# A two-layer graph kernel: in layer 1, TensorE picks two row tiles in place of one in every fourth step

## The chip, the cores and the metric

The kernel runs on one core of one Trainium2 chip. A core has five engines that run side by side and wait for each other by semaphores: TensorE (PE; matmuls into the eight banks of PSUM), VectorE (DVE), ScalarE (ACT), GpSimd (POOL) and SyncE (SP), and 16 DMA engines that move data between HBM and the on-chip memory SBUF. The metric is the device time of one execution in microseconds (us).

## The reference, cut to what matters

There are 12500 nodes with 32 features and 212500 edges, sorted by target. Layer 0 is an edge network with a segment maximum. Layer 1, the one that is changed, is a relational attention:

```python
x = h[src]                                    # one row of h for each edge
y = h[dst]
c = w_comp[etype]
msg = einsum('eb,ebo->eo', c, einsum('ei,bio->ebo', x, weight))
x_hat = x @ A1_w.T + A1_b
y_hat = y @ A2_w.T + A2_b + rel_emb[etype]
a = tanh(relu(sum(x_hat * y_hat, -1) / sqrt(32)))
nei = segment_sum(a[:, None] * msg, dst)
```

Each layer is added to its input, and a layer norm follows. The gather `h[src]` is where the change lies: how the rows of h come to the edges.

## The kernel before, in words

The edges lie in four streams. A step takes 512 edges of each, 2048 in all, as 16 row tiles of 128 edges with 32 features; each layer has 104 steps. A step's source rows come into one of two slots of the tile `xg1` in layer 1. The trace calls `xg1`, `xs` and the room of the hot tiles `rows_in`, because they share one tensor.

**How a row tile comes in.** Most come by a gather that GpSimd issues (L763): one indirect DMA for each row tile. Some are "hot": TensorE picks them with a one-hot matrix. The node of an edge is split into a class (which of 7 x 128 groups) and a lane (which of 14 nodes in the group). The one-hot matrix of the classes, 7 x 128 x 128 in bf16, is built by VectorE in layer 0 (`class_hot`), saved to HBM by SP (`hot_save`, L609) and loaded again in layer 1 (`hot_load`, L615). 21 matmuls (7 classes times 3 bf16 parts of h) give, for each edge, the 14 x 32 values of its group in one PSUM bank. VectorE multiplies them by a lane mask (`mask_hot`, L1369) and sums over the lanes (`add_hot`, L1375) into `xg1`. In layer 1 the last of the 16 row tiles is hot in each step from 6 to 101, so 15 are gathered.

**A step of layer 1.** Each engine runs a written-out order. For step s TensorE does, in this order:

- coefficients 0 and 1 (`coef`, L1591: matmuls that spread a coefficient over the features, in three banks in turn; each waits for the product that last read its bank)
- the score's sum (`score_sum`, L1608, bank 1), coefficient 2, the last messages of step s-1 (L1600), coefficient 3
- `compose` for step s+1 (L1617, banks 0 and 1), coefficient 4, the turn of the target rows (L1482), coefficient 5, `relate` for step s+1 (L1629, bank 5), coefficients 6 and 7
- the turn of the source rows of step s+1 (`source_turn`, L1648), which waits for its gathers and hot rows; coefficients 8 and 9
- hot piece 0 for step s+2 (`hot_rows`, L1664), messages of k = 0, coefficient 10, messages of k = 1, hot piece 1, coefficients 11 and 12, the key of step s+1 (`find_key`, L1672)
- hot piece 2, coefficient 13, hot piece 3, coefficient 14, hot piece 4, coefficient 15, hot piece 5, messages of k = 2, the turn of the sums of step s-1 (L1492)

`PIECES1` says where the 21 matmuls are cut into these six pieces. The first matmul of a tile waits for the hot load and for the query of step s+1, because the tile is summed in bank 5, which the query reads.

VectorE does in step s: the mask of the hot tile of step s+1, product 0 (`product`, L1340: the source features times a coefficient), the sum over the lanes, products 1 to 4, the weighing of the messages of step s-1 (L1347), product 5, a scan (L1353), product 6, a scan for step s+1 (L1235), product 7, the query of step s+1 (`find_query`, L1323), products 8 to 13, the lane mask of step s+2 (L1361), products 14 and 15, the score of step s+1 (`find_score`, L1329).

ScalarE copies what TensorE has turned to `xs` and stores it to HBM (L972). SP loads it back four times as `x4` (L723), which product 0 of the next step needs. SP's queue runs in order; for step s it loads indices, one-hot types, target rows, flags, the hot tile (L615), and then x4 for step s-2. GpSimd starts the gathers of step s when the slot has been turned and copied, that is two steps ahead of their use, and paces them by TensorE's coefficients.

Of the kernel before, what the change touches and what calls it, by code (L numbers as in the profile page):

```python
# [23 lines left out]
F = 32  # L24
# [34 lines left out]
LAST_HOT1 = STEPS - 2  # L59
FEW_HOT = STEPS - 5  # L60
PIECES = {1: (2, 4), 2: (5, 8), 3: (7, 12)}
HOTS1 = (1,)
PIECES1 = {1: (0, 0, 6, 11, 11, 16, 21)}
PICK = 14
CLASSES = NODES // (PICK * P)
HOT_COLS = STEPS * HOT
# [63 lines left out]
def hot1_count(n):  # L130

    if not FIRST_HOT1 <= n < LAST_HOT1:
        return 0
    return HOTS1[n % len(HOTS1)] if n < FEW_HOT else 1


def hot1_before(n):

    return sum(hot1_count(m) for m in range(n))
# [41 lines left out]
def build(nc, t):  # L181
    ctx = ExitStack()
    with ctx:
# [3 lines left out]
        def dram(name, shape, dt=fp32):  # L187
            return nc.dram_tensor(name, shape, dt, kind="Internal").ap()

        def sem(name):  # L190
            return ctx.enter_context(nc.semaphore(name))
# [13 lines left out]
        onehot_dram = dram("onehot_dram", [STEPS * TYPE_ROWS, STREAMS * LEN], bf16)  # L205
        hot_dram = dram("hot_dram", [STEPS * P, max(HOTS1) * CLASSES * P], bf16)

# [79 lines left out]
        def hot1(s):  # L287

            n = hot1_count(s.at)
            start = s.slot(2) * max(HOTS1) * CLASSES * P  # L290
            return hot1_room[:, start:start + n * CLASSES * P].rearrange("p (c t n) -> p c t n", c=CLASSES, t=n)
# [20 lines left out]
        def part(n):  # L312
            at[0] += n
            return late[:, at[0] - n:at[0]]
# [30 lines left out]
        h_low = part(NODE_COLS * F // 2).bitcast(bf16).rearrange("p (c n) -> p c n", c=CLASSES)  # L345
        picks1 = part(max(HOTS1) * PICK * F).rearrange("p (t f h) -> p t f h", f=F, h=PICK)

# [16 lines left out]
        bank = [psum[:, i, :] for i in range(8)]  # L364
        wmsg = bank[7]
        key = bank[0]
        hot_bank = [bank[6 + u][:, 0:PICK * F] for u in range(2)]
        hot_bank1 = [bank[5][:, 0:PICK * F]]

        def hot1_bank(s, t):  # L370

            return hot_bank1[t - hot1_count(s.at)]
# [65 lines left out]
        comp_ready = sem("comp_ready")  # L438
# [28 lines left out]
        hot1_read = sem("hot1_read")  # L467
# [12 lines left out]
        def wait_count(eng, s, semaphore, count):  # L480
            if s.known and count <= 0:
                return
            eng.wait_ge(semaphore, count)
# [39 lines left out]
        def wait_step(eng, s, semaphore, each=1, lag=0, more=0):  # L523

            wait_count(eng, s, semaphore, (s.at - lag + 1) * each + more)
# [31 lines left out]
        def _(sp):  # L557
# [47 lines left out]
            def hot_save(s):  # L605

                wait_step(sp, s, hot_built)
                n = max(HOTS1)
                sp.dma_start(hot_v[s.at][:, 0:n * CLASSES * P].rearrange("p (c t n) -> p c t n", c=CLASSES, t=n),  # L609
                             class_hot[s.slot(2)][:, :, HOT - n:HOT, :]).then_inc(hot_saved[s.slot(2)], 16)  # L610

# [42 lines left out]
            for n in range(PRE):  # L654
                hot_save(Step(PRE, 0, n))
                if n + 2 < PRE:
                    class_load(Step(PRE, 0, n + 2))
            sp.wait_ge(x_spread, 16 * NODE_COLS)

            def loads0(s):  # L660
                index = s.plus(PRE - 2)
                if index.exists() and (not s.known or index.at >= PRE + AHEAD):
                    index_load0(index)
                wait_step(sp, s, s_turned[0], lag=2)
                sp.dma_start(sp_in[:, s.slot(2)], spread_v[s.at]).then_inc(spread_in[0][s.slot(2)], 16)
                wait_step(sp, s, hid_done, each=2, lag=2)
                sp.dma_start(ea[:, s.slot(2), :], ea_v[s.at]).then_inc(ea_in[s.slot(2)], 16)
                keep_load(0, s)
                if hot(s.plus(4)):
                    class_load(s.plus(4))  # L670
                if hot(s.plus(2)):
                    hot_save(s.plus(2))
                if s.at >= 1:
                    types_load(s.plus(-1))
                if s.at >= 3:
                    onehot_save(s.plus(-3))
# [777 lines left out]
        def _(pe):  # L1454

            pe.wait_ge(lifted, 2)
            for k in range(NODE_COLS + 1):
# [5 lines left out]
                for q, half in enumerate(HALVES):  # L1463
                    if k >= 2:
                        pe.wait_ge((dve_counted, act_counted)[u], 2 * (k // 2) + q - 1)
                    for a in range(*half, 512):
                        b = min(a + 512, ROW)
# [137 lines left out]
            def score_sum(s):  # L1605

                wait_step(pe, s, score_ready)
                pe.matmul(bank[1][:, :], ones_blk[:, :], score, start=True, stop=True).then_inc(sum_done, 1)  # L1608

            def compose(s):  # L1610
# [41 lines left out]
            def hot_rows(s, piece):  # L1652

                each = CLASSES * PARTS
                a, b = PIECES1[hot1_count(s.at)][piece:piece + 2]
                for n in range(a, b):
                    t, rest = divmod(n, each)
                    if n == 0:
                        wait_in_hot = (s.earlier(2) - FIRST_HOT1 // 2 + 1) * 16
                        wait_count(pe, s, hot1_in[s.slot(2)], wait_in_hot)  # L1660
                    if rest == 0:
                        wait_step(pe, s, query_ready, lag=1)
                    c, q = divmod(rest, PARTS)
                    last_ = pe.matmul(hot1_bank(s, t), hot1(s)[:, c, t, :], h_parts[q][:, c, :],  # L1664
                                      start=rest == 0, stop=rest == each - 1)
                    if rest == each - 1:
                        last_.then_inc(hot1_done, 1)
# [10 lines left out]
            def step1(s):  # L1678
# [3 lines left out]
                turn = more and not turns_last and not picked_early(ahead)  # L1682
                coefs(s, 0, 2)
                score_sum(s)
                coef(s, 2)
                if behind.exists():
# [15 lines left out]
                if pick:  # L1702
                    hot_rows(later, 0)
# [3 lines left out]
                if pick:  # L1707
                    hot_rows(later, 1)
# [6 lines left out]
                if pick:  # L1715
                    hot_rows(later, 2)
# [151 lines left out]
```

## Time and profile before

| what | value |
|---|---|
| median of 3 runs | 4306.55 us (4303.88 to 4308.16) |
| the profiled execution | 4308.25 us |
| its span, first to last instruction | 4306.4 us |
| busy: PE / PE weight load / DVE / ACT / POOL | 86% / 39% / 64% / 28% / 74% |
| gathers of layer 1 (L763) | 1540, mean 946 ns |
| products of layer 1 (L1340) | 1664, mean 680 ns |
| hot matmuls of layer 1 (L1664) | 2016, mean 354 and 353 ns |

The busy shares run over both layers and the preparation. Layer 1 takes the second half of the span, from about 2200 us on. Matmuls are pipelined: the row of one shows its whole way through the array, so that rows overlap. The 0.3 us between two gathers are listed as idle by "issue": the engine waited for nothing that the profile shows.

### The profile page before, as it was taken

Reading aid. Unit: us, or ns where it says so; the run is one execution under the profiler, and the core shown is the slowest. Engines: PE = TensorE matmul, PEld = TensorE weight load, DVE = VectorE, ACT = ScalarE, POOL = GpSimd, SP = SyncE. Lnnn points to the kernel's source line nnn. Section 1 sums busy time; section 2 is a strip of 40 time slices with the busy share of each in tenths; the row PEclk is TensorE's granted clock in tenths of the full one; section 3 lists DMA queues with packets and bytes.
Section 4 is the critical chain, followed back from the end, with each engine's and each line's share of the span. In section 5 each row is a group of like instructions: output and inputs, shape, how many; then the busy total and the mean of one; then the engine's idle time right before and its main releaser. Section 6 shows DMA issues by size and latency. Waiting matters only on the chain.

```text
span 4306.4 us, 58419 instructions
## 1 busy us (share of the span) xinstructions
PE 3694.6 (86%) x20387; PEld 1663.0 (39%) x20607; DVE 2758.9 (64%) x4918; ACT 1197.9 (28%) x1615; POOL 3183.2 (74%) x3330
## 2 busy tenths in 40 slices
PE   7989999999999999941888989898889889988841
PEld 3444545545455455411433333333333333333311
DVE  8844444444444444426568888888888888888844
ACT  4424444444444434440011111111111111111111
POOL 7777777777777777767777777777777777777745
PEclk9999999999999999975899999999999999999965
DMA  8136565555555555551146666666666666666621
GB/s 341 26 92 154 137 143 136 141 138 141 140 138 141 138 140 142 134 133 35 28 112 168 169 172 168 163 169 168 164 163 171 167 165 162 173 167 164 159 60 32
DMA packets 526595, 608.78 MB, mean 141 GB/s; under 512 B 219555, under 2 KB 368576, under 8 KB 524128
## 3 DMA queue, kind: packets, MB, share of 16 engines
q1 hardware_dynamic: 374944, 439.68, 39.7%
q0 software_dynamic: 106432, 56.28, 8.5%
q10 hardware_dynamic: 44928, 109.07, 6.6%
q8 instruction: 166, 2.72, 0.3%
q14 instruction: 125, 1.02, 0.1%
HBM read 394.62 MB, written 210.03 MB: 140 GB/s over the span
## 4 chain that ended last, share of the span: by engine, by line
PE 59%; DVE 13%; DMA 10%; POOL 8%; issue 7%; ACT 2%; SPq 1%; ACTq 0%; DVEq 0%; POOLq 0%
PE psum L1506 24%; POOL rows_in L763 6%; PE psum L1542 6%; PE psum L1664 6%; DVE late L1340 5%; DMA late<-xs_dram 4%; PE psum L1600 4%; PE psum L1591 4%; DMA xs_dram<-rows_in 3%; PE psum L1744 3%; PE psum L1469 2%; POOL last_rows L763 2%; PE psum L1552 2%; PE psum L1492 2%; DVE dt_ L1235 2%
## 5 line engine op out<-in xcount | busy, mean ns | idle before, releaser
L763 POOL DMA_INDIRECT rows_in<-h_dram,src_idx x1540 | 1456.8, 946 | 476.3 <-issue 419.7
L763 POOL DMA_INDIRECT rows_in<-in_x_dram,src_idx x1392 | 1332.0, 957 | 435.7 <-issue 418.2
L1340 DVE TENSOR_TENSOR late<-late,psum 128x512 f32<-128x512 f32 x1664 | 1084.1, 680 | 360.7 <-PE psum L1591 217.4
L1506 PE MATMUL psum<-early,late 128*128 128x448 bf16 x5712 | 1130.8, 354 | 7.0 <-DVE late L1147 5.0
L1506 PEld LDWEIGHTS psum<-early,late 128*128 128x128 bf16 x5712 | 544.8, 98 | 625.3 <-issue 149.1
L1591 PE MATMUL psum<-comp,sel 128*128 128x512 bf16 x1461 | 512.2, 386 | 162.0 <-DVE late L1340 159.8
L1600 PE MATMUL psum<-late,basis 128*32 128x512 f32 x3328 | 449.0, 612 | 0.3 <-issue 0.3
L1147 DVE TENSOR_TENSOR late<-psum,lane_hot 128x448 f32<-128x448 f32 x272 | 169.9, 625 | 425.7 <-PE psum L1506 273.1
L1253 DVE TENSOR_TENSOR_SCAN scan<-fresh,scan,psum 128x512 f32<-128x512 bf16 x103 | 131.8, 1280 | 434.2 <-PE psum L1552 434.2
L1664 PE MATMUL psum<-x,rows_in 128*128 128x448 bf16 x1344 | 381.9, 354 | 0.0
L1591 PEld LDWEIGHTS psum<-comp,sel 128*128 128x128 bf16 x1664 | 155.6, 98 | 573.3 <-DVE late L1340 449.8
L993 ACT COPY early<-psum 128x512 f32<-128x512 f32 x104 | 61.0, 586 | 1053.1 <-PE psum L1492 1042.4
L1235 DVE TENSOR_TENSOR_SCAN dt_<-keep,dt_,psum 128x512 f32<-128x512 bf16 x206 | 263.0, 1277 | 60.7 <-PE psum L1482 60.3
L923 ACT ACTIVATE hid<-psum,b 128x512 f32<-128x512 f32 x208 | 131.7, 684 | 506.7 <-PE psum L1542 506.7
L1664 PE MATMUL psum<-late,rows_in 128*128 128x448 bf16 x672 | 237.5, 353 | 0.0
L1572 PE MATMUL psum<-ident,early 128*128 128x128 f32 (+1 forms) x56 | 15.6, 434 | 238.6 <-DVE early L1274 125.9
L1664 PEld LDWEIGHTS psum<-x,rows_in 128*128 128x128 bf16 x1344 | 123.9, 98 | 228.7 <-issue 139.1
L905 ACT ACTIVATE late<-late,row_id 96x2048 bf16<-96x2048 bf16 x104 | 207.2, 1992 | 0.4 <-ACT out L931 0.4
L909 ACT ACTIVATE late<-late 96x2048 bf16<-96x2048 bf16 x104 | 198.7, 1910 | 3.3
L1469 PE MATMUL psum<-late 128*128 128x512 bf16 (+1 forms) x775 | 148.4, 346 | 35.5 <-DVE late L1168 20.8
L1128 DVE TENSOR_SCALAR late<-late,class_id 128x384 bf16<-128x384 f16 (+2 forms) x728 | 175.1, 315 | 0.0
L1150 DVE TENSOR_REDUCE rows_in<-late 128x32 f32<-128x448 f32 x272 | 168.7, 620 | 9.4
(159 smaller groups left out, 4285.9 us busy)
## 6 DMA issues: line engine op xcount, KB each, us to landing
late<-xs_dram SPq DMA_DIRECT2D x416, 256.0 KB
sp_in<-spread SPq DMA_DIRECT2D x208, 256.0 KB
sum_rows<-early ACTq DMA_DIRECT2D x104, 512.0 KB, 2.7
late<-type_dram SPq DMA_DIRECT2D x104, 384.0 KB, 8.0
onehot_dram<-late SPq DMA_DIRECT2D x104, 384.0 KB
late<-onehot_dram SPq DMA_DIRECT2D x104, 384.0 KB
spread<-late SPq DMA_DIRECT2D x16, 1664.0 KB, 39.7
ea<-in_edge_t SPq DMA_DIRECT2D x104, 256.0 KB
```

The costliest lines, as they stand in the source:

```text
L763: pool.indirect_dma_start(out=out, out_offset=None, in_=table, in_offset=bass.IndirectOffsetOnAxis(ap=index, axis=0)).then_inc(done, 16)
L905: act.activation(gap[0:TYPE_ROWS, u], types[0:TYPE_ROWS, u], ACT.Square, bias=row_id[0:TYPE_ROWS, 0:1], scale=-1.0).then_inc(type_gap, 1)
L909: act.activation(onehot[0:TYPE_ROWS, u], gap[0:TYPE_ROWS, u], ACT.Relu, bias=1.0, scale=-1.0).then_inc(onehot_ready, 1)
L1128: last_ = dve.tensor_scalar(class_hot[u][:, c, tiles, :], class_in[:, u, tiles, :], class_id[:, c:c + 1], None, ALU.is_equal)
L1235: dve.tensor_tensor_scan(dt_[:, s.slot(2), :], keep[:, s.slot(4), :], bank[b][:, :], before(s, dt_), ALU.mult, ALU.add).then_inc(d_ready[n ...
L1340: dve.tensor_tensor(prod[:, n % G_BUFS, :], x4[:, s.slot(2), g, :], bank[C_BANK[n]][:, :], ALU.mult).then_inc(prod_ready, 1)
L1469: last_ = pe.matmul(found[u][:, a:b], below[:, k, :], lift_parts[:, c, a:b], start=c == 0, stop=c == 1)
L1506: last_ = pe.matmul(hot_bank[tile_slot(s, t)], class_hot[s.slot(2)][:, c, HOT - hot_tiles(s) + t, :], x_parts[:, c, q, :], start=c == 0 an ...
L1542: last_ = pe.matmul(bank[2 + q][:, :], w1[pair, (0, 2, 1)[k], :], rhs[pair, u, :], start=k == 0, stop=k == 2, tile_position=(2 * F * q, 0))
L1591: pe.matmul(bank[C_BANK[n]][:, :], sel[:, (g % 2) * KCH + k, :], comp[:, s.slot(2), g // 2, :], start=True, stop=True).then_inc(coef_done, 1)
L1600: last_ = pe.matmul(bank[7][F * g:F * g + F, :], basis[:, k, :], prod[:, (k * STREAMS + g) % G_BUFS, :], start=k == 0, stop=k == KCH - 1, ...
L1664: last_ = pe.matmul(hot1_bank(s, t), hot1(s)[:, c, t, :], h_parts[q][:, c, :], start=rest == 0, stop=rest == each - 1)
```

## The change

In every fourth step of layer 1 (n % 4 == 3, where 6 <= n < 99) two row tiles are hot in place of one, so that 14 are gathered. The table of pieces for such a step has seven matmuls in each of the six places. The bank of a tile is counted from the end: the last tile goes to bank 5 as before, the one ahead of it to bank 1, the bank of the score's sum. The two new waits belong to that bank: the score's sum waits until VectorE has masked the tile that lies there, and the first matmul of a tile waits until ScalarE has copied the composed coefficients of the step before. The save in layer 0 and the load in layer 1 carry two tiles for such a step; the room for them is there.

```diff
-HOTS1 = (1,)
-PIECES1 = {1: (0, 0, 6, 11, 11, 16, 21)}
+HOTS1 = (1, 1, 1, 2)
+PIECES1 = {1: (0, 0, 6, 11, 11, 16, 21), 2: (0, 7, 14, 21, 28, 35, 42)}
...
-        hot_bank1 = [bank[5][:, 0:PICK * F]]
+        hot_bank1 = [bank[b][:, 0:PICK * F] for b in (1, 5)]
...
             def hot_save(s):
 
                 wait_step(sp, s, hot_built)
-                n = max(HOTS1)
+                n = max(hot1_count(s.at), 1)
...
             def score_sum(s):
 
                 wait_step(pe, s, score_ready)
+                if hot1_count(s.at + 1) == 2:
+                    wait_count(pe, s, hot1_read, hot1_before(s.at + 1) + 1)
...
                     if rest == 0:
                         wait_step(pe, s, query_ready, lag=1)
+                        wait_step(pe, s, comp_ready, each=2, lag=1)
```

`hot1_count(n)` gives the number of hot tiles of step n, `hot1_before(n)` their number in all steps before it. Steps from 99 on have one tile as before, and `hot_rows` for step s+2 runs in step s.

## Rows read from the trace of the kernel before

**Rows 1.** Busy time of each engine in three stretches of layer 1.
```profile
core 0: us, PE busy (x) PEld busy (x) DVE busy (x) ACT busy (x) POOL busy (x), PEclk, DMA share, GB/s
2289.70:2658.92 369.22, 333.06 (x1982) 131.23 (x2021) 308.20 (x480) 69.25 (x121) 279.25 (x296) 1.00 0.65 169
2658.92:4009.55 1350.63, 1208.42 (x7130) 469.60 (x7272) 1104.19 (x1729) 249.34 (x433) 1021.22 (x1081) 1.00 0.64 167
4009.55:4120.54 110.99, 91.73 (x533) 33.07 (x543) 88.39 (x136) 21.03 (x37) 76.11 (x81) 0.98 0.53 136
```
**Rows 2.** VectorE's groups by line, 2289.7 to 4009.6 us.
```profile
L1340 DVE TENSOR_TENSOR late<-late,psum 128x512 f32<-128x512 f32 x1473 | 963.2, 680 | 308.4 <-PE psum L1591 207.1 <-DMA late<-xs_dram 92.1 <-PE psum L1600 7.6
...
L1375 DVE TENSOR_REDUCE rows_in<-late 128x32 f32<-128x448 f32 x92 | 56.3, 612 | 0.0
```
**Rows 3.** GpSimd's gathers in the same stretch.
```profile
L763 POOL DMA_INDIRECT rows_in<-h_dram,src_idx x1376 | 1301.7, 946 | 419.7 <-issue 373.3 <-PE psum L1591 30.5 <-ACT early L988 15.9
```
**Rows 4.** TensorE's timeline of step 20 (start, length, idle before).
```profile
2567.47 1.02 PE L1608 MATMUL psum<-hid,ones_blk 128*128 128x512 f32 x2
...
2570.74 0.60 PE L1482 MATMUL psum<-ident,sp_in 128*128 128x128 f32 x4 [0.16 <-issue]
...
2574.65 0.39 PE L1591 MATMUL psum<-comp,sel 128*128 128x512 bf16 x1 [1.15 <-DVE late L1340]
...
2576.42 0.39 PE L1591 MATMUL psum<-comp,sel 128*128 128x512 bf16 x1 [0.38 <-DVE late L1340]
2576.74 1.06 PE L1600 MATMUL psum<-late,basis 128*32 128x512 f32 x8
2577.73 0.55 PE L1664 MATMUL psum<-x,rows_in 128*128 128x448 bf16 x2
...
2578.88 0.38 PE L1591 MATMUL psum<-comp,sel 128*128 128x512 bf16 x1
...
2585.76 1.02 PE L1608 MATMUL psum<-hid,ones_blk 128*128 128x512 f32 x2
```
**Rows 5.** VectorE's timeline of the same step.
```profile
2568.06 0.61 DVE L1375 TENSOR_REDUCE rows_in<-late 128x32 f32<-128x448 f32 x1
2568.59 1.28 DVE L1340 TENSOR_TENSOR late<-late,psum 128x512 f32<-128x512 f32 x2
2570.06 0.69 DVE L1340 TENSOR_TENSOR late<-late,psum 128x512 f32<-128x512 f32 x1 [0.20 <-PE psum L1591]
2570.94 0.69 DVE L1340 TENSOR_TENSOR late<-late,psum 128x512 f32<-128x512 f32 x1 [0.18 <-PE psum L1591]
...
2575.70 0.66 DVE L1340 TENSOR_TENSOR late<-late,psum 128x512 f32<-128x512 f32 x1
2576.28 0.68 DVE L1323 TENSOR_TENSOR hid<-dt_,psum 128x512 f32<-128x512 f32 x1
...
2584.18 0.61 DVE L1369 TENSOR_TENSOR late<-psum,lane_hot 128x448 f32<-128x448 f32 x1
2585.75 0.69 DVE L1340 TENSOR_TENSOR late<-late,psum 128x512 f32<-128x512 f32 x1 [0.96 <-PE psum L1591]
```
**Rows 6.** What ended the idle time before the source turn (L1648): us, times.
```profile
  DMA rows_in<-h_dram,src_idx: 90.5, 102
```
**Rows 7.** Waits from 2289.7 to 2658.9 us: total, times, longest.
```profile
DVE late L1340 <- DMA late<-xs_dram: 9.0, 5, 2.6
```
**Rows 8.** SP's issues in step 20, and landing of layer 0's hot saves (L609).
```profile
2575.80 0.43 SPq L615 DMA_DIRECT2D rows_in<-hot_dram  x1
2578.54 1.75 SPq L723 DMA_DIRECT2D late<-xs_dram  x4
...
DMA to landing us min/median/max: 3.3/3.5/4.8
```
**Rows 9.** TensorE's timeline: two score sums near the end of layer 1.
```profile
4066.31 1.02 PE L1608 MATMUL psum<-hid,ones_blk 128*128 128x512 f32 x2
...
4081.78 1.02 PE L1608 MATMUL psum<-hid,ones_blk 128*128 128x512 f32 x2
```

## The prediction

> **What bounds the kernel now.** I read the profile from the whole to one step. The change touches layer 1 alone, so the stretch to read is its steady part, from score sum 5 at 2289.70 us to score sum 97 at 4009.55 us: 92 steps in 1719.85 us, 18.69 us each [rows 1, 2]. Layer 0 only saves two tiles in place of one in 23 steps.
>
> The first view to trust is GpSimd's. Its 1376 gathers of that stretch were busy 1301.7 us and had 419.7 us between them, nearly all "issue" [rows 3]: together the whole stretch, 1.251 us a gather. 15 gathers are 18.77 us, and steps 25 to 97 took 1350.63 / 72 = 18.76 us each [rows 1]. So GpSimd sets the pace of most of layer 1, and one gather less in four steps is worth up to 1.25 us.
>
> The second view says how far that can go. In the first 20 steps the gathers were ahead and TensorE did not wait for them; a step still took 18.29 us (2567.47 to 2585.76 in the one shown, 18.46 on average with some late loads) [rows 1, 4]. That is the loop of TensorE and VectorE alone, only 0.47 us under GpSimd's 18.77. The reader should follow it in the two timelines [rows 4, 5]. Coefficient 0 releases product 0; from there VectorE runs almost without a gap (0.20 and 0.18 us) to product 7 and the query, which ends at 2576.96. TensorE waits for it twice: 1.15 us ahead of coefficient 9 and 0.38 ahead of coefficient 10. From coefficient 10 at 2576.42 TensorE doesn't stop until coefficient 0 of the next step, and VectorE is the one that waits. The loop is a first half of VectorE and a second half of TensorE, and a hot tile lies in the second half.
>
> Waits of the stretch agree: TensorE lost 90.5 us to gathers [rows 6], VectorE 92.1 us to the four x4 loads [rows 2], and only 9.0 us of these in the first 20 steps [rows 7].
>
> **The change, part by part.** Target steps are n = 7, 11, ... 95: 23 of them. Their tiles are picked in steps 5, 9, ... 93.
>
> *Removed:* 23 gathers, 23 x 1.251 = 28.8 us of GpSimd. In four steps GpSimd needs 59 x 1.251 = 73.81 us, against 4 x 18.29 = 73.16 us of the TensorE-VectorE loop. So there are 0.65 us per four steps for all that the change adds before the loop becomes the bound.
>
> *Added to TensorE:* 21 matmuls in each of 23 steps. The mean of one is near 0.35 us, but they overlap: six of them and the step to coefficient 11 take 2578.88 - 2577.73 = 1.15 us, 0.19 each [rows 4], so 4.0 us for 21.
>
> *Where they stand* costs more than that. With one tile, piece 0 is empty and the first matmul comes after the messages of k = 1, at 2577.73, after the query. With two, piece 0 holds seven, directly behind coefficient 9, and its first one waits for the query of the same step (the old wait, kept for tile 0). In the step shown TensorE would reach it near 2574.9 and the query ends at 2576.96 [rows 4, 5]. Queued behind it are messages of k = 0 and coefficient 10, and VectorE's product 10 waits for that. So: query end 2576.96, a release of 0.06 (as from product 7's end at 2576.36 to coefficient 10), seven matmuls 1.34, eight message matmuls 0.99 (2576.74 to 2577.73): coefficient 10 at 2579.35 in place of 2576.42, 2.93 us late. The old stalls of 1.15 and 0.38 us, which might have hidden a piece, lie ahead of the query and are spent waiting.
>
> Behind coefficient 10 there are 35 hot matmuls in place of 21: 14 x 0.19 = 2.68 us, in the half where TensorE sets the end. Sum 5.6 us.
>
> *Added to VectorE:* one mask (0.61) and one reduce. The mask fits in the wait for coefficient 0 (0.96 us, [rows 5]); the reduce stands between products 0 and 1 and takes 0.53 us start to start (2568.06 to product 1), of which the gaps of 0.20 and 0.18 behind it hide 0.38: 0.15 left. A two-tile step thus costs 5.75 us more.
>
> *The two new waits:* the copies of the composed coefficients are read by coefficients that have long been issued by then, so that wait costs nothing behind the query's. The score sum's wait is for the mask of tile 0, which VectorE does directly behind the score, before the wait for coefficient 0; it is over before the score sum can start: nothing, and at most 0.61 us x 23 = 14 us if VectorE were the late one. What covers both is the longer TensorE half.
>
> *DMAs:* the hot load of a target step is 448 KB in place of 224. It goes on SP's queue ahead of the x4 loads, which it doesn't hold up in issue: issued at 2575.80, x4 at 2578.54 [rows 8]. No row says when it lands; the nearest is the save of the same 224 KB in layer 0, 3.5 us (3.3 to 4.8) [rows 8], thus near 2579.3, already over the x4 loads' start. Twice the bytes cost x4 between 0 and another 3.5 us; in the first stretch x4 was late in 5 of 20 steps [rows 7], so it has little to give, and most of the doubling runs beside the store that x4 waits for anyway: I take 0.4 us x 23 = 9 us and keep 80 us as the far end. The saves of layer 0 cost nothing: the slot is built anew two steps later, and 4.8 us doubled is 9.6; the work of those two steps covers it. Without that cover a build would wait a few us, 23 times.
>
> *Sum.* With the gathers no longer the bound: 92 x 18.29 = 1682.7; 23 x 5.75 = 132.3; late x4 loads as in the first stretch, (369.22 - 20 x 18.29) / 20 = 0.17 us in the 69 single steps = 11.8; doubled loads 9. Together 1836 us in place of 1720: +116 us. The tail from step 97, 110.99 us for six steps [rows 1], would start with gathers in hand: three steps at 18.29 and three without picks at no less than 15.46 (step 100, [rows 9]) are 101.3, so 0 to 10 us come back; I take 5. Net +111 us. The profiled execution took 4308.25 us, 1.85 over its span and 1.70 over the median of the three runs: 4308 + 111 = 4419, on the median's scale **4418 us**.
>
> **The rivals.**
>
> *GpSimd stays the bound* (the other side). The picks vanish in TensorE's gaps and 28.8 us of gathers are gone: 4280 us. It decides if a two-tile step costs under 0.65 us more. For it: TensorE is 90% busy, not full, and GpSimd is full. Against: the 18.29 us repeat in step after step without a wait for a gather, and even if every TensorE stall of that step (0.16 + 1.15 + 0.38) were filled, 4.0 - 1.7 = 2.3 us would remain.
>
> The Trainium skill, Perfetto Trace Analysis, section Identifying the Most-Contended Engine, says that matmul busy time is a bad measure of how full TensorE is and names weight-load time instead; that is 600.8 of 1719.9 us here, 35% [rows 1], which would leave room for the picks and speak for this rival's 4280 us. This trace speaks against it: TensorE's order, not its throughput, sets the second half of the loop.
>
> *The query's wait is mostly hidden.* If piece 0 started right behind coefficient 9, coefficient 10 would be 0.9 us late and the step 0.9 + 2.68 + 0.15 = 3.7 us longer: 23 x 2.05 = 47 us less than the forecast, 4371 us. With all stalls filled, 2.3 us a step, and neither late loads nor doubled ones: +53 - 37 - 10 = about 4314 us. Against it: the wait stands in the code, and VectorE's chain from coefficient 0 to the query has under 0.4 us of gaps.
>
> *The loads turn late as well.* Each doubled hot load pushes x4 by 2 us or more, at the head of the step where VectorE sets the pace: 23 x 1.6 = 37 us on top, 4455 us; at 3.5 us each, 4489.
>
> *No change:* 2.3 us or less per two-tile step and the whole tail regained: near 4306.
>
> **How the numbers follow.** Forecast 0.70 (4395 to 4445 by itself), wait hidden 0.12, late loads 0.08, GpSimd still the bound 0.06, no change 0.04. The range reaches down into the hidden wait and up into the late loads: 4365 to 4452. Under 0.2% either way is about what a measurement of this kernel can't tell from no change. Slower by more than that: 0.70 + 0.12 + 0.08 = 0.90; within: 0.04; faster: 0.06.
>
> **What would show it.** Score sums 18.3 us apart in three steps and about 24.0 in the fourth; in that step an idle TensorE of about 2 us before its first hot matmul, ended by the query (L1323); no wait of the source turn (L1648) for gathers; GpSimd with idle time that TensorE ends; no wait at the score sum. The granted clock was 1.00, the 2.4 GHz level, through stalls like these [rows 1] and should stay. The prediction is wrong if the two-tile step is under 19 us, if the source turn still waits for gathers, or if x4 is late in most steps.

## The result, and the profile after

The changed kernel takes 4436.39 us (median of 6 runs, 4430.81 to 4444.47) against 4306.55: the ratio is 1.0308, 95% interval 1.0298 to 1.0318, 130 us more. 4418 was forecast, with 4365 to 4452 as the range. The profiled execution took 4430.96 us, its span is 4429.2.

The same stretch as in [rows 1], from score sum 5 to score sum 97 (which is now L1610), and the tail behind it (columns as there):

```profile
2284.99:4134.31 1849.32, 1668.88 (x9776) 652.11 (x9775) 1443.79 (x2255) 318.51 (x553) 1287.19 (x1365) 0.98 0.61 158
4134.31:4243.69 109.38, 92.59 (x545) 33.45 (x543) 88.52 (x136) 21.03 (x37) 65.72 (x70) 0.98 0.53 136
```

The 92 steps take 1849.32 us in place of 1719.85, 129.5 more. The tail gives back 1.6 us and the stretch starts 4.7 us earlier, which makes all but 0.4 us of the 122.8 us between the two spans. The loss lies in the 92 steps, and the granted clock there is 0.98 where it was 1.00.

The same view for step 5 (two tiles), step 6 (one tile), and steps 9 and 13 (two tiles):

```profile
2284.99:2308.98 23.99, 20.83 (x123) 8.53 (x122) 16.17 (x26) 3.46 (x7) 18.20 (x20) 1.00 0.51 133
2308.98:2327.27 18.29, 16.76 (x102) 6.54 (x101) 15.82 (x25) 3.46 (x7) 9.95 (x12) 1.00 0.68 168
2363.97:2389.90 25.93, 22.52 (x123) 8.68 (x122) 16.00 (x26) 3.46 (x7) 19.53 (x22) 0.93 0.52 124
2444.77:2471.50 26.73, 23.57 (x124) 8.88 (x122) 16.09 (x26) 3.47 (x7) 18.53 (x20) 0.87 0.47 120
```

A single step takes 18.29 us, as foretold. A two-tile step takes 23.99 us where the clock stays at 1.00; that is so in four of the 23 (5, 49, 53, 69). The other 19 take 25.3 to 26.9 us at a lower mean clock. All 23 together are 586.6 us, 25.5 each.

TensorE's timeline of step 5 (start, length, idle time before) shows the forecast delay as drawn:

```profile
2284.99 1.02 PE L1610 MATMUL psum<-hid,ones_blk 128*128 128x512 f32 x2
...
2292.17 0.39 PE L1591 MATMUL psum<-comp,sel 128*128 128x512 bf16 x1 [1.14 <-DVE late L1340]
2294.58 0.54 PE L1667 MATMUL psum<-x,rows_in 128*128 128x448 bf16 x2 [2.02 <-issue]
...
2295.99 1.06 PE L1600 MATMUL psum<-late,basis 128*32 128x512 f32 x8
2296.99 0.39 PE L1591 MATMUL psum<-comp,sel 128*128 128x512 bf16 x1
...
2308.98 0.59 PE L1610 MATMUL psum<-hid,ones_blk 128*128 128x512 f32 x1
```

and VectorE's of the same moment shows what ended the 2.02 us, which the timeline above calls "issue", and what waits behind:

```profile
2293.79 0.68 DVE L1323 TENSOR_TENSOR hid<-dt_,psum 128x512 f32<-128x512 f32 x1
2297.19 0.69 DVE L1340 TENSOR_TENSOR late<-late,psum 128x512 f32<-128x512 f32 x1 [2.72 <-PE psum L1600]
```

The query ends at 2294.47, the first hot matmul starts at 2294.58, and VectorE's product 10 stands still until coefficient 10 has come. Coefficient 10 starts 12.00 us behind the score sum, where it was 8.95 [rows 4]: 3.05 late, 2.93 forecast. From it to the next score sum it is 11.99 us in place of 9.34: 2.65, 2.68 forecast.

The same place in step 13, at the lower clock:

```profile
2451.95 0.39 PE L1591 MATMUL psum<-comp,sel 128*128 128x512 bf16 x1 [1.14 <-DVE late L1340]
2454.36 0.90 PE L1667 MATMUL psum<-x,rows_in 128*128 128x448 bf16 x2 [2.02 <-issue]
...
2457.06 1.94 PE L1600 MATMUL psum<-late,basis 128*32 128x512 f32 x8
2458.93 0.61 PE L1591 MATMUL psum<-comp,sel 128*128 128x512 bf16 x1
```

and the busy times around it, with the granted clock (third number from the end):

```profile
2451.90:2453.40 1.50, 0.39 (x1) 0.10 (x1) 1.50 (x2) 0.42 (x1) 1.01 (x2) 1.00 1.03 303
2453.45:2460.20 6.75, 5.84 (x20) 1.38 (x24) 1.88 (x4) 0.00 (x0) 4.99 (x6) 0.50 0.91 223
2460.30:2471.50 11.20, 11.20 (x65) 5.23 (x57) 5.90 (x12) 0.23 (x1) 6.89 (x8) 1.00 0.14 24
```

Seven hot matmuls take 2.70 us here (2454.36 to 2457.06) and 1.41 in step 5, the messages of k = 0 take 1.87 in place of 1.00. That is the 1.2 GHz level (0.50), and it lasts into the messages of k = 1. What TensorE did before the clock fell: it waited 1.14 us, did one matmul and stood in the second wait, of 2.02.

GpSimd and the x4 loads in the 92 steps (the first row by line, the second from the waits: total, times, longest), and the matmul wait for gathers in the kernel before:

```profile
L763 POOL DMA_INDIRECT rows_in<-h_dram,src_idx x1365 | 1288.0, 944 | 562.4 <-issue 368.7 <-PE psum L1591 122.0 <-ACT early L988 71.7
DVE late L1340 <- DMA late<-xs_dram: 36.6, 25, 2.0
PE psum L1648 <- DMA rows_in<-h_dram,src_idx: 30.7, 39, 1.9
```

The gathers now wait for TensorE and ScalarE (idle 562.4 us, 419.7 before [rows 3]), and the source turn (L1650) waits for no gather at all, where its matmuls waited 30.7 us, 39 times, before. (The 90.5 us and 102 times of [rows 6] also count the idle time of the weight loads, 59.8 us and 63 times, which lies over the same waits.) So the saved gathers buy nothing: the pace has passed to the loop of TensorE and VectorE.

### The profile page after: what moved, and what is told of

It is laid out like the page before. It is cut to its first block, busy times and chain, and to the rows that moved or that the text cites. A ratio compares the mean times of both kernels' runs of the same rounds, so it can differ in the third digit from the quotient of the medians.

```text
span 4429.2 us, 59697 instructions
## 1 busy us (share of the span) xinstructions
PE 3822.6 (86%) x21090; PEld 1714.1 (39%) x21090; DVE 2789.6 (63%) x4964; ACT 1197.8 (27%) x1615; POOL 3153.4 (71%) x3307
## 4 chain that ended last, share of the span: by engine, by line
PE 69%; DVE 13%; issue 7%; DMA 5%; POOL 3%; ACT 1%; SPq 1%; ACTq 0%; DVEq 0%; POOLq 0%
PE psum L1506 25%; PE psum L1667 10%; PE psum L1542 6%; PE psum L1600 6%; PE psum L1591 5%; DVE late L1340 5%; DMA late<-xs_dram 3%; PE psum L1747 2%; PE psum L1469 2%; PE psum L1492 2%; PE psum L1552 2%; POOL last_rows L763 2%; DMA xs_dram<-rows_in 2%; DVE dt_ L1235 2%; PE psum L1675 2%
## 5 line engine op out<-in xcount | busy, mean ns | idle before, releaser
L763 POOL DMA_INDIRECT rows_in<-h_dram,src_idx x1517 | 1431.5, 944 | 616.9 <-issue 409.6
L1591 PE MATMUL psum<-comp,sel 128*128 128x512 bf16 x1664 | 579.8, 386 | 177.0 <-DVE late L1340 176.2
L1667 PE MATMUL psum<-x,rows_in 128*128 128x448 bf16 x1666 | 484.6, 361 | 46.5 <-issue 46.5
L1600 PE MATMUL psum<-late,basis 128*32 128x512 f32 x3328 | 458.1, 623 | 0.0
L1667 PE MATMUL psum<-late,rows_in 128*128 128x448 bf16 x833 | 299.7, 360 | 0.0
L1667 PEld LDWEIGHTS psum<-x,rows_in 128*128 128x128 bf16 x1666 | 157.3, 99 | 309.0 <-issue 191.9
```

What stands on the lines that cost most here:

```text
L763: pool.indirect_dma_start(out=out, out_offset=None, in_=table, in_offset=bass.IndirectOffsetOnAxis(ap=index, axis=0)).then_inc(done, 16)
L1591: pe.matmul(bank[C_BANK[n]][:, :], sel[:, (g % 2) * KCH + k, :], comp[:, s.slot(2), g // 2, :], start=True, stop=True).then_inc(coef_done, 1)
L1600: last_ = pe.matmul(bank[7][F * g:F * g + F, :], basis[:, k, :], prod[:, (k * STREAMS + g) % G_BUFS, :], start=k == 0, stop=k == KCH - 1, ...
```

## The experiments

All ratios are to the kernel before, run on the same chip (medians 4301.4 to 4302.1 us there, so times compare best by ratio).

| run | ratio (95% interval) | median us |
|---|---|---|
| query's wait off tile 0 | 1.0109 (1.0092 to 1.0126) | 4348.12 |
| nothing ahead of the query | 1.0132 (1.0115 to 1.0149) | 4358.40 |
| bank 1 and its waits alone | 1.0001 (0.9991 to 1.0010) | 4303.01 |
| wait filled with matmuls | 1.0232 (1.0215 to 1.0249) | 4404.01 |
| wide loads alone | 0.9999 (0.9990 to 1.0009) | 4301.10 |
| tile 0 in the stalls, two tiles in every fourth step | 0.9940 (0.9923 to 0.9956) | 4276.47 |
| the same, in every third step | 1.0007 (0.9997 to 1.0016) | 4305.60 |
| the same, one tile in each step | 1.0002 (0.9993 to 1.0012) | 4301.15 |
| every third step, half of x4 | 0.9901 (0.9884 to 0.9919) | 4259.21 |

The theory: the query's wait in piece 0, 14 more matmuls in TensorE's half, and a clock that falls over the wait (the dip). The rivals: the sheer amount of matmuls; the waits of bank 1; the doubled loads.

**The query's wait taken off tile 0.** Its bank is not the query's, so the wait can go without a race.

```diff
                     if rest == 0:
-                        wait_step(pe, s, query_ready, lag=1)
+                        if t == hot1_count(s.at) - 1:
+                            wait_step(pe, s, query_ready, lag=1)
                         wait_step(pe, s, comp_ready, each=2, lag=1)
```

> The changed kernel, but the first matmul of tile 0 (bank 1) no longer waits for the query; tile 1 (bank 5) still does. My theory (the query's wait in piece 0 delays coefficient 10 by 2.9 us, and the idle TensorE behind it loses its clock): the 2.0 us wait ahead of the first hot matmul goes, coefficient 10 is 0.9 us late in place of 2.9, two-tile steps take about 22.0 us in place of 25.5, the granted clock stays at 1.00 in them: 23 x 3.5 = 80 us less than the changed kernel, about 4356 us. Rival (it is the amount of matmuls on TensorE, wherever they stand): no more than 10 us less, 4426 or over. Rival (the waits of bank 1): unchanged, 4436.

It took 4348.12 us. Step 5, and TensorE's timeline in it:

```profile
2284.11:2305.92 21.81, 20.46 (x121) 8.57 (x122) 16.11 (x26) 3.46 (x7) 16.62 (x18) 1.00 0.57 145
```
```profile
2291.29 0.39 PE L1591 MATMUL psum<-comp,sel 128*128 128x512 bf16 x1 [1.14 <-DVE late L1340]
2291.51 0.54 PE L1668 MATMUL psum<-x,rows_in 128*128 128x448 bf16 x2
...
2292.93 1.07 PE L1600 MATMUL psum<-late,basis 128*32 128x512 f32 x8
2293.93 0.39 PE L1591 MATMUL psum<-comp,sel 128*128 128x512 bf16 x1
```

The hot matmuls follow coefficient 9 at once, coefficient 10 comes 9.82 us behind the score sum (0.87 late), and the clock stays at 1.00, here and in the other 22 two-tile steps. The wait and what hangs on it are worth 0.0199 of 4302, some 86 us, two thirds of the loss, with the number of matmuls unchanged.

**Nothing ahead of the query.** All waits stay; only the table is cut otherwise.

```diff
-PIECES1 = {1: (0, 0, 6, 11, 11, 16, 21), 2: (0, 7, 14, 21, 28, 35, 42)}
+PIECES1 = {1: (0, 0, 6, 11, 11, 16, 21), 2: (0, 0, 12, 22, 22, 32, 42)}
```

> The changed kernel with all waits, but the 42 matmuls of a two-tile step are cut 0, 12, 10, 0, 10, 10: nothing stands ahead of the query, as with one tile. My theory: no wait for the query, all 21 added matmuls lie in TensorE's half: 18.29 + 4.0 + 0.15 = 22.4 us for a two-tile step, clock at 1.00; 23 x 3.1 = 71 us less than the changed kernel, about 4365 us, still 59 us over the kernel before. Rival (amount of matmuls alone): 4426 or over. Rival (the waits of bank 1): unchanged, 4436.

It took 4358.40 us, and step 5 took 22.26 us at a clock of 1.00:

```profile
2282.51:2304.77 22.26, 20.47 (x120) 8.59 (x122) 16.09 (x26) 3.46 (x7) 16.98 (x18) 1.00 0.55 142
```

21 matmuls in TensorE's half cost 22.26 - 18.29 = 3.97 us, as 21 x 0.19 says. It is slower than the first run because none of its matmuls use the waits of the first half.

**Bank 1 and its waits alone.** The kernel before, with its one tile in bank 1.

```diff
-        hot_bank1 = [bank[5][:, 0:PICK * F]]
+        hot_bank1 = [bank[1][:, 0:PICK * F]]
...
                 wait_step(pe, s, score_ready)
+                if hot1_count(s.at + 1):
+                    wait_count(pe, s, hot1_read, hot1_before(s.at + 1) + 1)
...
                         wait_step(pe, s, query_ready, lag=1)
+                        wait_step(pe, s, comp_ready, each=2, lag=1)
```

> The kernel before with one hot tile in each step, but that tile is summed in bank 1 with both new waits in every step (96 of them) and bank 5 left to the relations. My theory: the mask is done before the score's sum can start and the copies long before, so both waits cost nothing: 4306 us, within 5. Rival (the score's sum waits for the mask, up to 0.6 us in each of 96 steps): up to 58 us more, 4364.

4303.01 us, ratio 1.0001: the two waits cost nothing, 96 times.

**The wait filled.** Nine matmuls more, into a bank that the next one overwrites.

```diff
                 for n in range(a, b):
...
+                    if n == 0 and hot1_count(s.at) == 2:
+                        wait_step(pe, s, comp_ready, each=2, lag=1)
+                        for m in range(9):
+                            pe.matmul(hot1_bank(s, 0), hot1(s)[:, m % CLASSES, 0, :], h_parts[m % 2][:, m % CLASSES, :],
+                                      start=True, stop=True)
```

> The changed kernel, but TensorE does nine more matmuls into bank 1 in each two-tile step while it would wait for the query; the first matmul of tile 0 overwrites what they leave, so they add work and take nothing away. My theory (order and clock are two costs): the query still sets coefficient 10, so a two-tile step takes the 24.0 us that it has at full clock, but the clock stays at 1.00: 23 x 1.5 = 35 us less than the changed kernel, about 4402 us, though there are 207 more matmuls. Rival (the clock's dips cost nothing, the extra 1.5 us come from late x4 loads): unchanged or slower, 4436 to 4445.

4404.01 us. With 207 matmuls more it is faster than the changed kernel by 0.0076 of 4302, 33 us (some 24 to 41, by the two intervals). Step 5, and what TensorE did in it:

```profile
2285.50:2309.46 23.96, 22.08 (x129) 9.37 (x131) 16.15 (x26) 3.46 (x7) 18.09 (x20) 1.00 0.54 133
```
```profile
2292.90 1.87 PE L1666 MATMUL psum<-x,rows_in 128*128 128x448 bf16 x9
2295.04 0.55 PE L1672 MATMUL psum<-x,rows_in 128*128 128x448 bf16 x2 [0.27 <-DVE hid L1323]
```

Here the profile names the query (L1323) as what ends the wait. The step is as long as at full clock in the changed kernel; what went is the dip, in all 23 two-tile steps (two steps with one tile, 24 and 32, have one). So the dip is a cost of its own, about 33 of 130 us, and comes from the wait.

**Wide loads alone.** The kernel before, every fourth hot save and load twice as wide; one of the two tiles is not used.

```diff
+def wide(n):
+
+    return 2 if FIRST_HOT1 <= n < FEW_HOT and n % 4 == 3 else 1
...
-                n = max(HOTS1)
+                n = wide(s.at)
...
-                             hot_v[s.at][:, 0:hot1_count(s.at) * CLASSES * P]).then_inc(hot1_in[s.slot(2)], 16)
+                             hot_v[s.at][:, 0:wide(s.at) * CLASSES * P]).then_inc(hot1_in[s.slot(2)], 16)
...
```

> The kernel before, one hot tile picked in each step and 15 gathers, but every fourth hot save and hot load carries two tiles, of which one is not used. My theory (the doubled loads are a small term): x4 is late by up to 0.4 us more in 23 steps, and partly inside the wait for gathers: 0 to 9 us over the kernel before, 4302 to 4311. Rival (the doubled load pushes x4 by 1.6 us or more each time): 37 us over, 4339.

4301.10 us, ratio 0.9999: in the kernel before, the doubled bytes cost nothing that can be measured, in layer 0 or 1. In layer 1 gathers set the pace of that kernel and can cover a late x4; what a late x4 costs the changed kernel is read from its own trace, below.

**Tile 0 in the stalls.** If place is what costs, a better place must win. Tile 0 goes to bank 1 in every step and doesn't wait for the query; its first pieces stand where TensorE waited for VectorE.

```diff
-PIECES1 = {1: (0, 0, 6, 11, 11, 16, 21), 2: (0, 7, 14, 21, 28, 35, 42)}
+PIECES1 = {1: (0, 6, 8, 11, 14, 14, 18, 21), 2: (0, 6, 8, 15, 22, 28, 35, 42)}
...
-            return hot_bank1[t - hot1_count(s.at)]
+            return hot_bank1[t]
...
-                if hot1_count(s.at + 1) == 2:
+                if hot1_count(s.at + 1):
...
-                coefs(s, 8, 10)
+                coef(s, 8)
+                if pick:
+                    hot_rows(later, 0)
+                coef(s, 9)
                 if pick:
-                    hot_rows(later, 0)
+                    hot_rows(later, 1)
```

The other pieces keep their places, with numbers one higher. Tile 0 waits for the copies alone, tile 1 for the query alone.

> Two tiles in every fourth step as in the changed kernel, but tile 0 is summed in bank 1 in every step, has no wait for the query, and its first 6 matmuls stand between coefficients 8 and 9 and 2 more behind coefficient 9, where TensorE waited 1.15 and 0.38 us for VectorE. My theory (place, not amount): 8 x 0.19 = 1.5 us leave TensorE's half, a single step of the loop takes 16.8 us and a two-tile step 20.9; four take 71.3 us, under the 73.81 us of 59 gathers, so GpSimd sets the pace again and the saved gathers count: 92 steps of 18.45 us, 22 us less than the kernel before, about 4280 us. Rival (two tiles cost TensorE too much wherever they stand): over 4310. Rival (saved gathers are worth nothing): 4302.

> As the run with tile 0 in the stalls, but two tiles in every third step. My theory: 44 gathers in three steps are 55.04 us, the loop 2 x 16.8 + 20.9 = 54.5: GpSimd still sets the pace, 18.35 us a step, 31 us less than the kernel before, about 4271 us, with little margin left. Rival (the loop or the x4 loads bind first): slower than the run with every fourth step, 4280 or more.

> One hot tile in each step and 15 gathers as in the kernel before, but the tile is summed in bank 1 and 8 of its 21 matmuls stand in TensorE's two waits. My theory: the loop falls from 18.29 to 16.8 us, the gathers of 18.77 us set every step now, and the source turn waits for them in nearly each; the time falls by the few us of slack in the tail at most: 4294 to 4304. Rival (the loop, not the gathers, set the kernel before): 92 x 1.5 = 138 us less, 4165.

With two tiles in every fourth step it took 4276.47 us, ratio 0.9940: faster than both kernels, and under the kernel before by 26 us of the 28.8 that 23 gathers are worth. A single step of it that waits for nothing, and the gathers from 2290 to 4000 us:

```profile
3040.92:3057.69 16.77, 16.76 (x102) 6.39 (x101) 15.70 (x25) 3.46 (x7) 12.75 (x14) 1.00 0.69 183
```
```profile
L763 POOL DMA_INDIRECT rows_in<-h_dram,src_idx x1366 | 1289.1, 944 | 421.5 <-issue 388.9 <-PE psum L1591 23.5 <-ACT early L988 9.2
```

The step is 16.77 us for 16.8 worked out, and 1289.1 + 421.5 fill the stretch: GpSimd sets the pace again.

With one tile in each step the time is that of the kernel before, 1.0002, and the gathers fill the 1710 us there too:

```profile
L763 POOL DMA_INDIRECT rows_in<-h_dram,src_idx x1371 | 1293.9, 944 | 417.8 <-issue 383.1 <-ACT early L988 18.6 <-PE psum L1591 16.2
```

So a shorter loop alone is worth nothing while 15 gathers are issued, and it was the gathers that bound the kernel before.

Two tiles in every third step gave 1.0007, and the expectation of 4271 fell. Three steps of it, and what VectorE's products waited for:

```profile
3055.42:3072.20 16.78, 16.77 (x102) 6.40 (x101) 15.70 (x25) 3.46 (x7) 11.91 (x13) 1.00 0.72 182
3072.20:3089.76 17.56, 17.00 (x102) 6.52 (x101) 15.14 (x24) 3.46 (x7) 13.20 (x14) 1.00 0.73 189
3089.76:3111.50 21.74, 21.04 (x123) 8.64 (x122) 15.91 (x26) 3.46 (x7) 16.36 (x18) 1.00 0.60 148
```
```profile
L1340 DVE TENSOR_TENSOR late<-late,psum 128x512 f32<-128x512 f32 x1455 | 937.8, 679 | 294.2 <-PE psum L1591 175.2 <-DMA late<-xs_dram 112.3 <-PE psum L1600 5.7
```

They take 56.08 us where the loop was worked out at 54.5 and the gathers at 55.04; the first of the three is at the loop's 16.8, and the other two are behind it. The gathers are not what is late: the source turn waits for none in this run. The row of VectorE names the x4 loads, 112.3 us; x4 is late in the other two steps of the three and never in the first. The row alone shows no bound, since the run with every fourth step has nearly the same wait (110.7 us) at the pace of its gathers.

**Half of x4.** As the run with every third step, but each x4 load brings half of its columns and the products use that half twice.

```diff
-                    sp.dma_start(x4[F * k:F * k + F, u, :, :], xs_dram[u].rearrange("(g f) n -> f g n", f=F)
+                    sp.dma_start(x4[F * k:F * k + F, u, :, 0:LEN // 2],
+                                 xs_dram[u].rearrange("(g f) n -> f g n", f=F)[:, :, 0:LEN // 2]
```

> The run with two tiles in every third step and tile 0 in the stalls, but each x4 load brings half of its columns (half the bytes, the same number of issues), and the products use that half twice, so the messages of the other half are left out. My theory now (that run fell because x4 lands after coefficient 0, 52 times and 112 us in 1710): x4 lands earlier by up to half of its transfer, most of those 112 us go, gathers or the loop of 54.5 us in three steps set the pace: 30 us less than that run or more, 4265 to 4280. Rival (the TensorE-VectorE loop of that run is longer than I worked out): within 10 us of that run, 4296 to 4310.

4259.21 us, ratio 0.9901, 46 us under the run with whole loads, and 6 us below the expected range. The wait is gone, and the gathers fill the 1710 us again:

```profile
L1341 DVE TENSOR_TENSOR late<-late,psum 128x512 f32<-128x512 f32 x1490 | 971.9, 680 | 244.7 <-PE psum L1593 228.3 <-PE psum L1602 14.2 <-DMA late<-xs_dram 2.0
L764 POOL DMA_INDIRECT rows_in<-h_dram,src_idx x1368 | 1293.0, 945 | 418.8 <-issue 395.3 <-PE psum L1593 14.9 <-ACT early L989 8.6
```

So behind the loop and the gathers a third bound lies close: store, load and use of x4. That is shown for this variant. Half the bytes also lower the busy share of the DMA engines, from 0.67 to 0.52 in the 1710 us; whether x4's own transfer or the freer engines bring it in time was not separated, and how the chain could be shortened with all its bytes was not tried.

## Why the prediction was right, step by step

- *GpSimd binds before, and the loop lies just under it*: right. The single steps of the changed kernel take 18.29 us, and the run with one tile in the stalls shows that the loop did not bind before. One reading beside it was wrong: TensorE did not lose 90.5 us to gathers but 30.7, as said above; no term of the sum hangs on it.
- *The query's wait in piece 0, 2.93 us, and 14 matmuls behind it, 2.68*: right, 3.05 and 2.65 in step 5. The whole two-tile step at full clock costs 23.99 - 18.29 = 5.70 us more, which is their sum; 5.75 were forecast. In 23 steps that is 131 us. The run without the wait and the run with another table show each part for itself.
- *The new waits cost nothing*: right, by the run with bank 1 alone; in the changed kernel, too, no idle time stands ahead of the score's sum (L1610).
- *One reduce, 0.15 us*: it cost nothing. The tiles of step 5 are reduced in step 6:

```profile
2309.57 1.14 DVE L1375 TENSOR_REDUCE rows_in<-late 128x32 f32<-128x448 f32 x2
2313.05 0.69 DVE L1347 SCALAR_TENSOR_TENSOR psum<-xt,psum 128x512 f32<-128x512 f32 x1
```

  The weighing (L1347) starts 4.07 us behind the score sum there, as in the kernel before [rows 4, 5], and step 6 takes 18.29 us: VectorE's gaps hide the second reduce whole.
- *The clock stays at 1.00*: wrong, and this is the largest term that the forecast left out. The prediction took the mean of a long stretch of the kernel before, 1.00, for the clock in each stall. Read step by step, that trace has the clock fall in three of its 92 steps (8, 51 and 77), where TensorE had a wait of 1.4 to 1.9 us. Step 77:

```profile
3633.36:3653.77 20.41, 18.15 (x100) 6.99 (x101) 15.35 (x24) 3.46 (x7) 15.27 (x17) 0.92 0.62 156
```

  The stalls of step 20 come to 1.69 us (0.16, 1.15 and 0.38); a two-tile step waits 1.14 and 2.02 with a single matmul between, and in 19 of 23 the clock fell to 1.2 GHz. These 23 steps are 34.8 us over 23 x 23.99, of which about 33 are left when late x4 loads (below) are taken off; by the filled wait it is 33 as well.
- *Late x4 loads, 12 us, and the doubled load, 9 us*: too high. 92 x 18.29 + 131 leave 35.5 us of the 1849.32, and the clock takes about 33 of them. x4 is still late in 17 of the 23 two-tile steps, whose x4 follows a doubled hot load, and in 8 of the 69 others. But only three single steps are longer for it (18.40, 18.72 and 18.43), 0.7 us in all, and by the same measure the two-tile steps lose an estimated 1.7: about 2.4 us in place of 21.
- *The tail gives 5 us back*: it gave 1.6. On the other hand the stretch starts 4.7 us earlier, which was not forecast.

In sum, the terms of the order and the amount were right, a term of 33 us was missing, and the load terms were some 18 us too dear, so that the 92 steps came out only 13 us over the 1836 forecast. That these errors cancel in part is luck. The profiled execution is 12 us over the 4419 forecast for it; the rest of the 18 us comes from the median itself, which lies 5.4 us over that execution where the prediction took it 1.7 under.

The rivals: GpSimd as the bound fell, since the source turn waits for no gather. The hidden wait fell by the 2.02 us in the timeline. The late loads fell by the 2.4 us above. The Trainium skill (Perfetto Trace Analysis, Identifying the Most-Contended Engine) judges TensorE's headroom by weight-load time and the share of peak arithmetic, not by matmul busy time. The trace agrees that there was room: weight loads take 652.11 of 1849.32 us after the change, 35% as before. But only an order that uses the room gets at it: the same 42 matmuls cost 130 us in one place and let 26 us be gained in another.

The fall of the clock over waits is described in the Trainium skill, TensorE: Matmul & The Clock Gate, section HAM oscillation: a TensorE that waits for a load drops to the lower rate and starts the next work slowly. This trace agrees, with seven matmuls in 2.70 us after the waits and in 1.41 where the clock held. The waits of the page's own case are longer than the two here, 1.14 and 2.02 us with one matmul between them; these brought the clock down in most of the steps, and in four they did not.

## What to carry to other kernels

When a kernel is bound by one engine, read from steps in which that engine was ahead how long the next loop is: here 18.29 us under 18.77, so that the saved gather paid in full only if the two-tile step grew by less than 0.65 us, and it grew by 5.70. Work added to a shared in-order engine is priced by what is queued behind it: matmuls that wait, ahead of work that others need, cost the wait, and matmuls moved into a gap of that engine shorten the step (18.29 to 16.77 us here). And a new wait beside an old one can cost the clock as well: read the granted clock step by step, not as the mean of a stretch, and fill the wait or, better, move the work out of it.

## What the runs showed of the hardware

That the clock fell in 19 steps and held in four was not expected. Twelve of the 19 have the same two waits as the four (1.14 or 1.15 us, and 2.02); in the other seven the first wait is 1.26 to 1.38 us. What tells the twelve from the four stays open. Work added in the wait, 207 matmuls, made the kernel 33 us faster.
